# A transformer block on one core: two value products and the feed-forward product split, PSUM banks fixed by kind, two steps moved

## The reference

```python
H, hd = 16, 16                       # x: (16, 512, 256)
xn = _layernorm(x)
q, k, v = split_heads(xn @ w_qkv.T + b_qkv)
att = q @ k.T / sqrt(hd) + hope_bias(pos_independent)
att = softmax(where(causal, att, -inf))
attn = (att @ v) @ w_proj.T + b_proj
y = fp8(xn) @ fp8(kernel) * scales + bias
return x + attn + y
```

## Time and profile before

| what | value |
|---|---|
| median of 3 runs | 769.26 us (769.14 to 769.72) |
| the profiled execution, own time | 769.2 us |
| its span in the trace | 767.2 us |
| one body, MT of (0, 3) to the next pass's | 446.61 - 402.15 = 44.46 us |
| PE, DVE, ACT, POOL busy | 96%, 83%, 76%, 69% |
| granted TensorE clock, mean | 0.99 of full speed |

### The profile page before, as it was taken

One profiled execution on the slowest core, in us unless ns is written; L12 is line 12 of the kernel. 1 busy time (PEld: TensorE's weight loads), 2 busy tenths in 40 slices (PEclk: granted clock), 3 DMA queues, 4 the chain that ended last, 5 costly groups with the idle time before them and its releaser, 6 DMA issues.

```text
span 767.2 us, 23128 instructions
## 1 busy us (share of the span) xinstructions
PE 738.7 (96%) x6285; PEld 475.1 (62%) x6285; DVE 634.6 (83%) x2401; ACT 586.1 (76%) x1263; POOL 532.4 (69%) x525
## 2 busy tenths in 40 slices
PE   7989999999999999999999999999999999999987
PEld 4656556666765666566566656666665666666555
DVE  4898798889989888988988898898988889888613
ACT  4557888787888878788887878878787888877662
POOL 7445767786777778776777868677776867767571
PEclk9999999999999999999999999999999999999889
DMA  5442353435335433533544253244425334443201
GB/s 181 150 152 103 128 176 142 139 118 178 117 138 174 153 127 118 184 128 121 174 153 141 112 187 136 108 170 152 158 95 193 133 120 153 160 148 108 88 32 62
DMA packets 55313, 105.65 MB, mean 138 GB/s; under 512 B 10421, under 2 KB 30389, under 8 KB 55285
## 3 DMA queue, kind: packets, MB, share of 16 engines
q1 hardware_dynamic: 53968, 104.52, 38.3%
q10 hardware_dynamic: 1316, 0.80, 0.4%
HBM read 18.42 MB, written 8.90 MB: 36 GB/s over the span
## 4 chain that ended last, share of the span: by engine, by line
PE 68%; ACT 11%; DVE 8%; issue 6%; DMA 2%; SPq 2%; DVEq 1%; ACTq 1%; POOLq 0%; POOL 0%
PE misc_a L560 13%; PE misc_a L674 10%; PE misc_b L560 9%; PE scoreT_b L648 9%; PE scoreT_a L648 5%; PE score_c L625 4%; PE misc_b L674 3%; ACT probs L1013 3%; PE score_a L625 2%; PE scoreT_b L651 2%; ACT qk_parts L901 2%; ACT attn_hi L992 2%; DVE row_max L1101 2%; SPq L351 1%; ACT out_T L986 1%
## 5 line engine op out<-in xcount | busy, mean ns | idle before, releaser
L1324 POOL TENSOR_SCALAR_AFFINE_SELECT probs<-probs 128x512 f32<-128x512 f32 x256 | 161.1, 640 | 185.7 <-ACT probs L1013 184.0
L1101 DVE CUSTOM_DVE_ANT_0 score_b<-score_b,causal_mask_q 128x384 f32<-128x384 f32 (+3 forms) x321 | 162.7, 523 | 80.6 <-PE score_b L625 80.3
L1101 DVE CUSTOM_DVE_ANT_0 score_a<-score_a,causal_mask_q 128x512 f32<-128x512 f32 x319 | 174.6, 563 | 2.9 <-PE score_a L625 2.8
L1101 DVE CUSTOM_DVE_ANT_0 score_c<-score_c,causal_mask_q 128x256 f32<-128x256 f32 (+3 forms) x384 | 172.0, 475 | 0.1
L1013 ACT ACTIVATE probs<-scoreT_b 128x384 f32<-128x384 f32 (+1 forms) x256 | 131.8, 515 | 44.7 <-PE scoreT_b L651 21.2
L1013 ACT ACTIVATE probs<-scoreT_a 128x512 f32<-128x512 f32 (+1 forms) x256 | 142.6, 557 | 9.3 <-PE scoreT_a L651 8.0
L1101 DVE DVE_READ_ACCUMULATOR2_ANT row_max<- 128x1 f32 x1024 | 142.8, 139 | 0.0
L1013 ACT ACTIVATE probs<-scoreT_c 128x384 f32<-128x384 f32 (+1 forms) x256 | 133.3, 521 | 1.5 <-PE scoreT_a L648 0.9
L674 PE MATMUL misc_a<-probs,v_ones 128*32 128x128 f32 (+3 forms) x1536 | 124.1, 441 | 3.5 <-DVE xnT_lo L1083 1.3
L648 PE MATMUL scoreT_b<-stacks 64*128 64x384 f32 (+3 forms) x320 | 120.6, 396 | 1.6 <-ACT probs L1013 1.5
L625 PE MATMUL score_b<-stacks 64*128 64x384 f32 (+3 forms) x321 | 116.0, 394 | 0.0
(11 more groups left out here) (238 smaller groups left out, 1937.4 us busy)
## 6 DMA issues: line engine op xcount, KB each, us to landing
stacks<-qk_parts SPq DMA_DIRECT2D x128, 512.0 KB, 3.7
x_ring<-in_L_attn_x SPq DMA_DIRECT2D x16, 512.0 KB, 3.6
attn<-out_T SPq DMA_DIRECT2D x63, 128.0 KB, 2.6
xn<-recips SPq DMA_DIRECT2D x31, 256.0 KB
out<-x_ring SPq DMA_DIRECT2D x15, 512.0 KB, 3.0
stacks<-neg_max_T SPq DMA_DIRECT2D x128, 4.0 KB
low_features<-neg_max_T SPq DMA_DIRECT2D x126, 4.0 KB
low_features<-probs SPq DMA_DIRECT2D x8, 128.0 KB, 4.3
```

The lines of the kernel that those rows point to most:

```text
L1101: last = V.tensor_tensor_reduce(bank, bank, CMQ[:, T - w:T], 1.0, LEAST, ALU.add, ALU.max, MX[:, g % 2, 8 * h + 4 + qt:8 * h + 5 + qt])
L1324: last = GP.affine_select(out=d, in_=d, compare_op=ALU.is_ge, fill=0.0, base=0, pattern=[[0, HU], [1, P]], channel_multiplier=-1)
```

## The change

Nothing of the arithmetic changes, and all sums keep their order. What changes is where jobs stand.

- PV of groups 1 and 2 are split like the others: tile 0 at (2, 0) and (3, 0), tiles 1 to 3 at (2, 3) and (3, 3). MT stands behind tile 1 there; in groups 0 and 3 it stays where it was.
- FF's first half stays at (2, 0), behind PV's tile 0. The second half goes to (2, 6), ahead of V, on PE and on ACT, where its evacuation comes after the exponential of that chunk and before V's.
- PJ's first half at (3, 0) comes behind PV's tile 0. DVE's addition of it goes from (3, 1) to (3, 0).
- The banks are fixed by kind: PV always misc_a, MT, FF and PJ always misc_b, QK, V and T one in each.

```diff
-PV_AT = [(1, 0), (2, 3), (3, 3), (0, 0)]
-
-PV_REST_AT = {0: (1, 3), 3: (0, 3)}
+PV_AT = [(1, 0), (2, 0), (3, 0), (0, 0)]
+
+PV_REST_AT = [(1, 3), (2, 3), (3, 3), (0, 3)]
-FF_AT = [(2, 0), (2, 0)]
+FF_AT = [(2, 0), (2, 6)]
-FF_OUT_AT = [(2, 0), (2, 1)]
-RESULT_AT = [(3, 1), (3, 6)]
+FF_OUT_AT = [(2, 0), (2, 6)]
+RESULT_AT = [(3, 0), (3, 6)]
...
-MISC_BANK = {job: n % 2 for n, job in enumerate(ORDER)}
+MISC_BANK = {(kind, i): bank for kind, banks in (("PV", (0, 0, 0, 0)), ("MT", (1, 1, 1, 1)), ("QK", (0, 1, 0, 1)), ("FF", (1, 1)),
+                                                 ("V", (0, 1)), ("PJ", (1, 1)), ("T", (0, 1))) for i, bank in enumerate(banks)}
...
-                elif then and g < 3:
+                elif then and g == 0:
                     job_MT(*then)
...
-                    if j == 0 and then:
+                    if j == 1 and then and g in (1, 2):
                         job_MT(*then)
...
                             if (g, k) == PV_AT[pg]:
-                                pv(pb, pg, range(1) if pg in PV_REST_AT else range(TT), None if pg in PV_REST_AT else then)
-                            if pg in PV_REST_AT and (g, k) == PV_REST_AT[pg]:
+                                pv(pb, pg, range(1), None)
+                            if (g, k) == PV_REST_AT[pg]:
                                 pv(pb, pg, range(1, TT), then)
```

More of the change, by code:

```diff
@@ L82 @@
 FIRST_CHUNKS = [0, 1, 4, 5, 8, 9, 2, 3, 6, 7, 10, 11]
-KINDS = ("PV", "MT", "QK", "V", "FF", "PJ", "T")
+KINDS = ("PV", "MT", "QK", "FF", "V", "PJ", "T")
 ORDER = [(KINDS[kind], i) for _, kind, i in sorted((at, kind, i) for kind, ats in enumerate(
-    (PV_AT, MT_AT, QK_AT, V_AT, FF_AT, PJ_AT, [T_AT, T_AT])) for i, at in enumerate(ats))]
-assert len(ORDER) % 2 == 0
-MISC_BANK = {job: n % 2 for n, job in enumerate(ORDER)}
+    (PV_AT, MT_AT, QK_AT, FF_AT, V_AT, PJ_AT, [T_AT, T_AT])) for i, at in enumerate(ats))]
+MISC_BANK = {(kind, i): bank for kind, banks in (("PV", (0, 0, 0, 0)), ("MT", (1, 1, 1, 1)), ("QK", (0, 1, 0, 1)), ("FF", (1, 1)),
+                                                 ("V", (0, 1)), ("PJ", (1, 1)), ("T", (0, 1))) for i, bank in enumerate(banks)}
 MASKED = -1.0e30
@@ L818, in body @@
                                 job_QK(b + 1, i)
+                        for i in due(FF_AT, g, k):
+                            job_FF(b, i)
+                        if not last:
                             for i in due(V_AT, g, k):
                                 job_V(b + 1, i)
-                        for i in due(FF_AT, g, k):
-                            job_FF(b, i)
                         if not first:
@@ L1015, in body @@
                             max_T(b, 1)
+                        for i in due(FF_OUT_AT, g, k):
+                            act.wait_ge(ff_ready, 2 * b + i + 1)
+                            if i == 0 and not last:
+                                act.wait_ge(qz_done, b + 2)
+                            A(Y1[:, 2 * i:2 * i + 2, :], misc_of("FF", i)[:, :].rearrange("p (t c) -> p t c", c=C),
+                              ACT.Identity, scale=SC[:, 3:4]).then_inc(y1_ready, 1)
                         if not last:
@@ L1031, in body @@
                                 attn_hi(b - 1, ct)
[L1032 to L1037, removed]
             body(0, True, False, True)
```

## The result

| | before | after |
|---|---|---|
| median, us | 769.2 (768.73 to 769.72, 4 runs) | 774.5 (772.42 to 776.86, 4 runs) |
| ratio, with its 95% interval | | 1.0077 [1.0049, 1.0105] |
| profiled execution, span | 769.2, 767.2 | 772.42, 770.7 |
| distance of one steady pass to the next | 44.45 | 44.62 |

A forecast was written before the change was run, and what follows sets the result against it. TensorE, busy 96% of the span, was taken as the bound. 13 x 0.35 = +4.5 us, less 0.6 in pass 0 and 0.1 in pass 14, gave +3.8 on 769.2: 773.0 us, range 766.5 to 775.5.

The forecast's parts named there:

- the mechanism named: ScalarE runs late from the exponential of (3,1) to T0's copy, delaying PV3's tile 0: the pass ends 0.35 us later.
- Third group: TensorE from the third group's first job to V0: 0.0 us change, between -0.36 and +0.15.
- The new wait of about 0.5 at (2, 6): The score matmul of (2,6) waits about 0.5 us for VectorE's maximum of (2,3), replacing the waits removed.
- Fourth group, PE: TensorE in the fourth group, PV2's tile 0 ahead of PJ's first half: +0.02 to +0.08 us at chunk 7.
- Fourth group, ACT: ScalarE's exponential of (3,1) starts 1.04 us later, idle time absorbs 0.67, T0's bf16 copy is late: +0.35 a pass.
- the other place: ScalarE's idle time before the exponential at 439.73, taken as about 0.14 us of the 0.67 absorbed.
- The drain at each switch of tile shape: TensorE at the four new tile-shape changes: up to 0.8 us a pass if each drained; not counted in the sum.
- Passes 0, 14 and 15: First pass -0.6 us, pass 14 -0.1, pass 15 0, beside +4.5 for passes 1 to 13.
- (a): No change: VectorE not in the way at (2,6) and ACT cancels the gain, or neither decides; 768.4 or 769.3, chance 0.20.
- (b): Faster: ACT and VectorE catch up, TensorE keeps the third group's 0.36 us; 764.6 us, chance 0.18.
- (c): Slower by more: drain at each switch or the late maxima's load adds 0.2 to 0.3 a pass; 776, chance 0.06.

The follow-up runs named there:

- e8: e2 with VectorE's three quantisation steps on 8 of 512 columns only, most of the quantisation left out: 760.71 us, ratio 0.9913.
- e9: Changed kernel with attn_hi at (2,4) and (2,5), first normalisation at (2,8), second quantisation step at (2,3): 761.9 us, ratio 0.9932.
- e2: Changed kernel with ScalarE's two attn_hi copies at (2,4) and (2,5) instead of (2,2) and (2,3): 769.52 us, ratio 1.0022.
- e6: Kernel before with only the fourth group's part of the change (PV2 and its MT split, result at (3,0)): 768.62 us, ratio 1.0012.
- e1: The changed kernel timed again without an edit, on another chip: 780.64 us, ratio 1.0169.
- e7: Kernel before with only the third group's part of the change (PV1 split, second feed-forward half at (2,6)): 784.76 us, ratio 1.025.
- e10: e9 with the first two normalisations at (3,0) instead of (2,8) and (3,3): 759.05 us, ratio 0.9891.
- e4: Changed kernel with VectorE's last quantisation step at (2,4) instead of (2,3), so that attn_lo starts first: 782.11 us, one execution.

## Why the prediction was right, and where it was not

The forecast was 773.0, within 766.5 to 775.5, slower at 0.62; measured was 774.5. The sign and the mechanism named were right. That the sum came out near was luck: one term was twice too large, and another was missing.

- **Third group.** V0 was to stay where it was, +0.00 (-0.36 to +0.15); it is 0.04 later behind the group's first job, and the group takes 11.22 against 11.18. Chunk 4 was to start 0.9 sooner and starts 0.81 sooner. The new wait of about 0.5 at (2, 6) is there, 0.60 in the weight loads, and e8 and e9 show that VectorE's queue sets it. Right.
- **Fourth group, PE.** Chunk 1 was to lie 3.0 behind chunk 0: 2.98. MT waits for max_hi and starts 436.20 - 434.41 = 1.79 behind chunk 1, against 435.95 - 434.08 = 1.87 predicted. PE at chunk 7 was to be +0.02 to +0.08 and is 0.05 ahead; a small miss without weight, as ACT decides.
- **Fourth group, ACT: the mis-sized term.** The chain exponential, T0's copy, T0's subtraction, PV3 is in the rows of after, of e2 and of e6. Its size was 0.35 a pass; it is 0.17. The exponential of (3, 1) starts 434.94 - 426.98 = 7.96 behind V0 against 7.00 before, so +0.96 where 1.04 was taken; and from it to T0's copy it is 441.91 - 434.94 = 6.97 against 7.77 before, so that 0.80 is absorbed where 0.67 was. Together 0.16 instead of 0.37. The rows hold the reason. The row of the kernel before that stands ahead of out_T:

```profile
436.12 0.34 ACT L914 ACTIVATE neg_max_T<-misc_a,part_sign 32x128 fp32r<-32x128 f32 x1
```

  From it to out_T it was 436.99 - 436.12 = 0.87, and it is 437.75 - 437.50 = 0.25: 0.62 absorbed, where the prediction took the printed idle time, 0.53. The 0.09 more is that an instruction which is not kept waiting starts about 0.1 before the recorded end of the one ahead of it (437.50 + 0.34 = 437.84), so a wait costs that much more than the view prints. At the other place the prediction took a distance, and its 0.14 came out (0.49 from 439.83 to the exponential at 440.32 in after, 0.63 before). The last 0.04 are distances a hundredth or two shorter; out_T takes 0.57 instead of 0.60, and why is not settled.
- **The term left out: the collision.** Nothing in the prediction priced attn_lo against the quantisation step. It took what VectorE does up to 425.65 as not dependent on the moved work; VectorE's start against GpSimd's did depend on it. Their rows of before, 0.32 apart and each longer than its undisturbed time, would have shown that they already met. It gives about 1.6 us in the profiled execution, about 11 of the 12.9 us on e1's chip (e1 less e2), and most of the spread.
- **The drain at each switch of tile shape** was not borne out: with t0 in front, the feed-forward product of after enters 1.00 behind t0 and (2, 1) 0.54 behind that, as the rows of before had it, and e7's undisturbed passes, with two of the four new changes, are no longer than before's. The entry of 0.43 into t0, from the scores' tiles of 64*128 to those of 128*32, is no price of the 32 columns either: into the feed-forward product with its 128*128 it is the same 0.43. Weight loads of the kernel before at (2, 0):

```profile
419.98 0.18 PEld L625 LDWEIGHTS score_a<-stacks 64*128 64x128 f32 x1
420.41 0.33 PEld L603 LDWEIGHTS misc_a<-ffn_w_q,xq 128*128 128x128 bf16 x4 [0.25 <-issue]
```

- **Passes 0, 14 and 15.** Pass 0 was to be 0.6 shorter and is 0.62 longer (41.92 against 41.30). A stretch at the lower clock lies in it, which e2 does not have; there the pass takes 40.73, 0.57 shorter, as predicted. Windows of after (columns as above):

```profile
80.00:84.00 4.00, 3.10 (x22) 2.26 (x18) 3.50 (x16) 4.00 (x11) 3.03 (x3) 0.83 0.07 26
84.00:88.00 4.00, 4.00 (x29) 2.21 (x28) 2.79 (x12) 2.97 (x8) 1.06 (x2) 0.74 0.42 161
88.00:92.00 4.00, 4.00 (x43) 2.41 (x40) 3.62 (x12) 3.39 (x9) 4.00 (x4) 1.00 0.31 123
```

  So the 3.5 us of the profiled execution's span are: a first pass that starts 1.0 sooner, -0.57 and 1.19 of clock in pass 0, +1.6 in passes 1 to 13 (where +4.5 was summed), +1.77 in pass 14 (where -0.1 was summed), +0.5 in the last. The prediction's +3.8 was near by its size and not by its parts.
- **The rivals.** Without the collision the change is (a) in all but name: e2 is at 1.0022, 1.7 us, the edge of what can be told. So the sign itself, at the size measured, is owed to what was left out. (b) asked that ACT make up over 0.3 of its 0.37; it made up 0.21. Its gain is real, but it needs the moves of e10. (c) fell: neither of its two causes shows, though e1's chip gave more than its 776.

The profiled run of after, at 772.42, is also a warning against one execution: e1's, of the same program, was at 787.54.

## What to carry to other kernels

Before two independent instructions of VectorE and GpSimd like these, each with two inputs in SBUF, are shifted against each other by some tenths of a microsecond, read their starts in every pass: a step that is longer than its undisturbed length by 0.2 or 0.3 already meets its neighbour, and a move that brought the starts within 0.1 turned that into a loss of 1.6 to 3.1 us in some passes here (the larger ones with the clock's fall behind it), differently in each run. A split that feeds TensorE sooner moves the wait to the engines which read its results, so lay out their queues (here three table entries, 1.0077 to 1.0169 without them, 0.9891 with them) before judging it. Printed idle time in a queue understates what a late start can make up, here by 0.09 at one wait: take the distance from start to start instead, and compare it with that of instructions which aren't kept waiting.

## What the runs showed of the hardware

- A VectorE step of 0.69 us took up to 2.93 when attn_lo (2.38 alone) had started 0.00 to 0.06 us before it (after, e1, e7), and 2.40 when 0.52 before it (e4): in every pass it ended 0.55 after attn_lo did. With VectorE first, attn_lo ended 2.24 to 2.26 after the step in every pass of before, after, e1, e6 and e7: it took 2.94 when both started together, and 2.82 when VectorE led by 0.35, where the step took 0.89 to 1.03. The lengthening of the first one in that last case is not explained.
- An activation of ScalarE that had nothing to wait for started about 0.1 us before the recorded end of the one ahead of it.
- The granted clock fell to the lower level for about 3.4 us after four of e1's eight collisions and three of e7's eight, and after none of e4's fourteen. The same fall stands in pass 0 of after, without a collision, and cost 1.2. The runs don't settle what tells these places apart.
